# One transformer block on one core: the last 512 rows normalised, projected and routed as one part of four tiles instead of two parts of two

## The reference, cut to what matters

```
mod = (silu(c) @ wmod).reshape(1, 6, 1, -1)          # sa, ca, ga, sb, cb, gb
h = layernorm(x) * (1 + ca) + sa
q, k, v = split(einsum('bse,ehd->bshd', h, w_qkv), 3)
a = softmax(mask(q k^T / 8)) v                        # 16 heads of 64
x = x + ga * einsum('bshd,hde->bse', a, w_out)
h = layernorm(x) * (1 + cb) + sb
e = argmax(h @ Wr.T + br)                             # one expert of 8 for each row
x = x + gb * (relu(h @ W1[e].T + b1[e]) @ W2[e].T + b2[e])
```

## Time and profile before

| | us |
|---|---|
| median of three runs | 985.71 |
| lowest and highest run | 983.54, 986.17 |
| the profiled execution's own time | 979.31 |
| span of the profiled execution | 977.5 |
| PE busy | 949.9 (97% of the span) |
| DVE busy | 710.1 (73%) |
| ACT busy | 675.8 (69%) |
| POOL busy | 110.3 (11%) |

### The profile page before, as it was taken

How to read it: one execution, slowest core, us unless ns; L and a number is a source line. 1 busy time by engine, 2 the same in 40 slices (tenths; PEclk the granted TensorE clock), 3 DMA queues, 4 the chain that set the end, 5 groups by cost and what they waited for, 6 DMA issues and landing times.

```text
span 977.5 us, 19704 instructions
## 1 busy us (share of the span) xinstructions
PE 949.9 (97%) x6851; PEld 746.1 (76%) x6851; DVE 710.1 (73%) x2363; ACT 675.8 (69%) x1245; POOL 110.3 (11%) x125
## 2 busy tenths in 40 slices
PE   4999999999999999999999999999999999999797
PEld 3678777777777777777777777777777777878697
DVE  6987658784887758784887668874887578986564
ACT  3877658675877768666875768666766677764485
POOL 0200011000100010000100010000100010202244
PEclk9999999999999999999999999999999999999899
DMA  3011100110011100110011000110010000005220
GB/s 82 16 32 26 31 16 20 50 26 20 15 31 26 31 18 18 50 27 20 15 32 50 15 15 13 49 26 20 15 31 18 12 8 11 27 14 175 67 64 27
DMA packets 56003, 30.79 MB, mean 31 GB/s; under 512 B 12455, under 2 KB 53203, under 8 KB 55906
## 3 DMA queue, kind: packets, MB, share of 16 engines
q1 hardware_dynamic: 54658, 27.41, 10.5%
q0 software_dynamic: 1248, 2.13, 0.7%
HBM read 18.21 MB, written 11.77 MB: 31 GB/s over the span
## 4 chain that ended last, share of the span: by engine, by line
PE 96%; DVE 2%; DMA 1%; SPq 0%; ACT 0%; issue 0%; POOLq 0%; POOL 0%; DVEq 0%; ACTq 0%
PE ps L812 27%; PE ps L843 25%; PE ps L825 25%; PE ps L791 5%; PE ps L795 3%; PE ps L856 3%; PE ps L967 2%; PE ps L978 2%; DMA x_sb<-in_L_attn_x_dram 0%; PE ps L942 0%; PE ps L896 0%; PE ps L939 0%; PE ps L958 0%; PE ps L765 0%; DVE k_both L1168 0%; DVE q_both L1164 0%
## 5 line engine op out<-in xcount | busy, mean ns | idle before, releaser
L1032 ACT ACTIVATE probs<-probs,neg_max 128x128 f32<-128x128 f32 (+15 forms) x256 | 309.0, 1210 | 98.0 <-DVE neg_max L1192 96.3
L812 PE MATMUL ps<-k_both,q_both 128*128 128x512 f32 (+2 forms) x1280 | 360.9, 398 | 2.1 <-DVE q_both L1164 1.1
L825 PE MATMUL ps<-ident,probs 128*128 128x128 f32 x2176 | 297.4, 273 | 0.2
L1040 ACT COPY pT<-ps 128x512 f32<-128x512 f32 (+1 forms) x428 | 227.6, 565 | 87.4 <-PE ps L825 81.2
L825 PEld LDWEIGHTS ps<-ident,probs 128*128 128x128 f32 x2176 | 254.7, 140 | 42.4 <-issue 9.9
L1185 DVE TENSOR_SCALAR_CACHE_REDUCE probs<-ps 128x512 f32<-128x512 f32 (+1 forms) x384 | 247.2, 665 | 10.3 <-PE ps L812 8.7
L843 PE MATMUL ps<-pT,v_sb 128*64 128x256 f32 (+1 forms) x2304 | 250.0, 370 | 0.0
L812 PEld LDWEIGHTS ps<-k_both,q_both 128*128 128x128 f32 x1280 | 208.5, 190 | 50.3 <-issue 27.6
L843 PEld LDWEIGHTS ps<-pT,v_sb 128*64 128x64 f32 x2304 | 157.4, 137 | 80.6 <-issue 9.2
L708 POOL CAST k_both<-k_both 64x1024 fp32r<-64x1024 f32 x64 | 66.5, 1038 | 746.3 <-DVE k_both L1168 744.2
L1188 DVE CUSTOM_DVE_ANT_0 probs<-ps,causal 128x256 f32<-128x256 f32 (+3 forms) x256 | 130.6, 510 | 2.1 <-PE ps L812 1.2
(11 more groups left out here) (143 smaller groups left out, 569.2 us busy)
## 6 DMA issues: line engine op xcount, KB each, us to landing
x_sorted<-blank SPq DMA_DIRECT2D x19, 458.5 KB, 5.1
rinv_b<-spread_rows SPq DMA_DIRECT2D x128, 64.0 KB, 2.6
spread_rows<-rinv_rows SPq DMA_DIRECT2D x256, 0.5 KB
probs<-in_L_ffn_W_dram SPq DMA_DIRECT2D x1, 2048.0 KB, 11.9
w_pair<-in_L_attn_w_qkv_dram SPq DMA_DIRECT2D x24, 64.0 KB, 2.2
hT<-x_sorted SPq DMA_DIRECT2D x23, 65.5 KB, 1.8
x_sb<-in_L_attn_x_dram SPq DMA_DIRECT2D x4, 256.0 KB, 4.3
wo_pair<-in_L_attn_w_out_dram SPq DMA_DIRECT2D x8, 64.0 KB, 1.9
```

Source lines behind the costliest of these rows:

```text
L812: m = pe.matmul(ps_ring[:, s.bank, 0:w], q_split[r % 2][:, q0:q0 + P], k_split[r % 2][:, part, k0:k0 + w], start=(part == 0), stop=(part = ...
L825: m = pe.transpose(ps_turn[:, n % TURN_BANKS, P * r:P * r + P], probs[:, g % 2, r, j * P:j * P + P], ident[:])
L1032: act.activation(row, row, ACT.Exp, bias=neg_max[:, g, r:r + 1], accum_out=row_sum[:, g, r:r + 1]).then_inc(exp_done, 1)
L1040: act.copy(pT[:, n % PT_SLOTS, lo:BANK], ps_turn[:, n % TURN_BANKS, lo:BANK]).then_inc(turn_taken[n % TURN_BANKS], 1)
```

## The change

The last pair has the same four parts of four tiles as the other pairs. The former parts of tiles 12 and 13 and of tiles 14 and 15 are one part. The load of the spread reciprocals of the very last group had a semaphore of its own, since the last part waited for it alone; it now counts on the same one as its neighbour.

```
 def parts_of(p):
 
-    return [(0, 4), (4, 4), (8, 4), (12, 4)] if p < PAIRS - 1 else [(0, 4), (4, 4), (8, 4), (12, 2), (14, 2)]
+    return [(0, 4), (4, 4), (8, 4), (12, 4)]
```

```
                                      spread_rows[n:n + 1, h::2, :].broadcast_to([D, 2, P])
-                                     ).then_inc(spread_in[part % 2 if n < PAIRS * GROUPS - 1 else 2], 16)
+                                     ).then_inc(spread_in[part % 2], 16)
```

## The result

The changed kernel takes 987.63 us (median of 20 runs, 985.4 to 989.45), the kernel before 985.65 us (20 runs, 983.28 to 987.22, on the same chip). The ratio is 1.0022 with a 95% interval of 1.0015 to 1.0028: **2.2 us slower (1.5 to 2.8)**, inside the 0.3% that the prediction called no change, and 0.4 us from the forecast of +2.6.

What follows compares the result with a forecast made beforehand. PE was taken to bound the kernel, then a DVE-PE chain up to the first gather. Products -1.6, dependent steps +4.0 and scatter +0.2 gave +2.6 us on the 985.71 median: 988.3 us, range 985.0 to 991.5.

Steps and rivals of the forecast that it cites:

- Term 1: Last attention group: PE loses the former fourth part's pieces, so the last product ends earlier; -1.6 us.
- The price of a switch: PE, last group: going from a batch of products to turns costs 0.15 us; three more switches, +0.45 us.
- Term 2: Dependent steps behind the last product, up to DVE's ends: longer with four tiles than two; +4.0 us.
- the cover for the longer pick: Between route and rank: two expert-weight turns on PE (1.9 us) hide a pick grown by about 0.6; nothing charged.
- Term 3: Before the first gather: POOL sends four scatters behind the last rank, and the fourth now comes last; +0.2 us.
- The second layer's weights: Their load and three turns precede the turn of normalised rows on PE; nothing charged, at most 0.1 us.
- The clock: PE's idle before the first tiles grows from 5.7 to 6.8 us; low restart in both, nothing charged, bounds ±2.1.
- The signs of being wrong: Copy waits above 0.5 us, weights holding normalised rows, clock rise over 5 us after restart, or gather before 923.5.
- Short batches: Last group: PE waits for copies in each batch, leaving no gain in products; +4.2 us, 989.9; chance 0.14.
- Late scatter: Before the first gather: the four scatters land up to 7.1 us after issue; +7.3 us, 993.0; chance 0.04.
- Slow restart: After PE's idle before the first tiles: clock rises 4.3 us later; +4.7 us, 990.4; chance 0.08.
- Fixed costs of DVE: Root's tiny DVE steps run once less, saving 2.45 us; +0.15 us, 985.9; chance 0.14.

Runs made afterwards that it cites:

- two-batch order: Changed kernel with the last attention group's turns and products in two long batches instead of four; 1.0034 of the kernel before.
- the run with two scatters: Changed kernel with the last two of its sixteen scatters (tiles 14 and 15) left out; 1.0021 of the kernel before.
- the second trace of after: Second profile of the changed kernel, run again unedited; in its timed comparison 1.0032 of the kernel before.
- the run with PE kept busy: Kernel before, with 40 turns of the identity on PE while it waits for the first tiles; 0.9988 of the kernel before.

## Why the prediction was right

The median forecast was 988.3 and came as 987.63; the shift was put at +2.6, measured at +2.2 in the first comparison, +3.1 in the second, and +2.86 from slots to gather in the traces.

*Term 1, -1.6, measured -1.36.* The pieces taken out are 18 matmuls of 145, as listed, and the chain of before has them at the 2.25 us that I took. The price of a switch and the wait of 0.2 for copies were near: four batches instead of two cost 0.57 in all, which is two switches at 0.15 and 0.27 of wait, 0.07 more than put down. The other 0.17 lies in the turns that stay. The two-batch order is 1.93 us shorter than before where my prices give 2.10 (2.25 less one switch): its 62 turns take 7.30 us on the chain and took 6.98 before, of which I had counted one switch. Why a turn is dearer in the long rows is open.

*Term 2, +4.0, measured +4.07.* It holds in parts: to the normalised rows +2.5 (my sum 2.37), to the slots +1.15 (my sum 1.14), total +0.43 (0.46). Charging the root's tiny steps alike for two and four columns was right, and so was the cover for the longer pick: between those two turns (L942 x16) and rank PE doesn't stand.

*Term 3, +0.2, measured +0.15 to +0.2.* The fourth scatter does come last, but the small sum is partly luck. Against the chain of DVE and SP it comes last by 0.35 us, as the run with two scatters shows; that chain is 0.2 shorter than before, since DVE's step L1320 no longer runs beside POOL's scatter, and I had not seen that. The scatter landed 2.35 and 2.43 us after issue where I took 2.6, and left 3.54 us behind the start of the ends, where my instants make it 3.4.

*The second layer's weights: charged nothing, at most 0.1.* In the change it cost next to nothing (0.02 us between the two traces). But I had read the earlier trace rows as "landed by 909.02" and did not ask what that is worth to term 1: it bounds it. Without the longer steps of term 2, 0.8 us of term 1 would have been lost, and with two batches 1.2 us were. The step was right for this order and would have failed for the next one.

*The clock: nothing.* PE's idle time grew from 5.7 to 6.7 us, as reckoned, and the restart is at the low level in both, against, in the second trace of after:
```profile
920.30:927.04 6.74, 0.04 (x2) 0.04 (x1) 3.68 (x11) 0.58 (x1) 2.14 (x3) 0.86 0.21 56
927.04:931.30 4.26, 4.13 (x17) 3.54 (x18) 1.58 (x5) 2.01 (x7) 0.00 (x0) 0.50 0.32 72
```
The clock is back at 1.00 from about 932.0 on, some 5.0 us behind the restart, where in the two traces of before it was some 4.1 and 4.7; from the gather to the end it is 55.7 against 55.6 and 55.5.

*The signs of being wrong.* Three of the four that I had named showed or came close. PE did wait for copies for more than 0.5 us in one of the two traces of the change (1.37), in the other the turn of the normalised rows had the weights' landing on its chain, and the clock's rise stood at the 5 us named. The forecast holds because the first is not in every execution, the second costs 0.02 us and the third 0.1 to 0.2, not because they were ruled out.

*The rivals.* Short batches: term 1 would have been 0; it was -1.36, and two batches bring only 0.57 more. It fell. Late scatter: landing 2.4, not 7.1. It fell. (Its +4.9 is 0.2 too much: the bound in term 3 gives +4.7.) Slow restart: it fell, and the run with PE kept busy prices what the low clock takes there at 1.2 us. Fixed costs of DVE: they gave nothing back; in the last group DVE was idle even more (5.62 of 14.88 us busy, against 9.75 of 16.23 in the earlier trace rows) and PE the bound all along.

What the prediction did not foresee is the spread of one execution: the first profile's hole in the second batch of turns hid term 1 completely, so that slots to gather was +4.5 there. With that trace alone term 1 would have read +0.2, and the "short batches" rival would have looked true. Such a hole stands in 3 of the 7 traces with four batches (1.06, 1.19 and 1.37 us) and in 1 of the 7 with two; in the first three it stands in the second batch of turns, at 7.1 to 7.4 us behind the third part's slots. It may be that short batches give a late copy more chance to stop PE, but these numbers don't decide that, and what delays the copies was not found.

## What to carry to other kernels

Merging two small parts into one pays only what leaves the bounding engine's queue ahead of the last dependency, and costs the second part's width in every step behind it; here 1.4 us against 4.1. To gain from such a merge, do it for parts whose steps are still covered by other work, not for the last one. When products come earlier, ask for each load behind them how much margin it had, and before reordering loads, what other engine will then run its big instruction at whose small steps. Profile twice before explaining a difference of a few microseconds: one stall that came and went was as large as the term in question.

## What the hardware showed that I had not expected

- A multiply on POOL of 128x1024 elements (2.36 us) holds a DVE step of two columns with two SBUF inputs for 2.27 us (0.16 alone) and a copy of four columns for 1.98 us (0.17 alone), while DVE's steps that read PSUM run beside it at full speed. POOL's issue of a scatter does the same in small: DVE's step L1320 takes 0.38 us beside it and 0.17 without.
- A stop of PE of 2.12 us was followed by a mean granted clock of 0.58 over the eight microseconds from 910 to 918, so that L942 x16 took 3.56 us and not 1.89. A stop of 2.86 us in another kernel left the clock at 1.00.
- The weights' load landed 10.8 to 12.75 us after its issue when it left second, and 15.1 to 15.9 when it left first, sharing the queues with the other big loads: sent 6.6 to 7.2 us earlier, it landed 2.1 to 4.2 us earlier. The load that stands first behind another big one holds SP's queue for 5.4 to 7.1 us, be it the 512 KB or the 2 MB.
